# The rounding-down step of a fixed-point feed-forward block: an integer round trip, or a ladder of compares and subtractions

## The reference, cut to what matters

```python
x = L0_attn_x                                    # (4, 4096, 1024) fp32
x = x + _layernorm(_L0_attn_ref(_layernorm(x), Wq, Wk, Wv, Wo, bo))
x = x + _layernorm(_L0_ffn_ref(_layernorm(x), w1, b1, w2, b2))

def _L0_ffn_ref(x, w1, b1, w2, b2):              # w1 (1024, 4096), w2 (4096, 1024)
    h = x @ w1 + b1
    h = float2fix(h, 8)                          # round(h * 256) / 256
    h = pwlin_gelu_basic(h, 8, 8)                # 32 straight pieces of width 0.25 on [-4, 4]
    h = float2fix(h, 8)
    out = h @ w2 + b2
    return float2fix(out, 8)
```

## Time and profile before

| | us |
|---|---|
| median of 3 runs (7682.74 to 7688.47) | 7682.78 |
| the profiled execution | 7684.76 |
| its span, slowest core (core 4) | 7682.8 |
| spans of the 8 cores | 7658.8 to 7682.8 |
| VectorE busy | 2179.4 (28% of the span) |
| TensorE matmuls busy | 3020.9 (39%) |
| ScalarE busy | 1439.9 (19%) |

### The profile page before, as it was taken

How to read it: one execution, slowest core, us unless ns; L and a number is a source line. 1 busy time by engine, 2 the same in 40 slices (tenths; PEclk the granted TensorE clock), 3 DMA queues, 4 the chain that set the end, 5 groups by cost and what they waited for, 6 DMA issues and landing times.

```text
span 7682.8 us, 34600 instructions; the slowest of 8 cores (7658.8 to 7682.8 us)
## 1 busy us (share of the span) xinstructions
PE 3020.9 (39%) x7361; PEld 857.5 (11%) x7440; DVE 2179.4 (28%) x3496; ACT 1439.9 (19%) x2201; POOL 289.5 (4%) x484
## 2 busy tenths in 40 slices
PE   3434444444434444444444465222233332221443
PEld 1111000000011110000000111000000010000110
DVE  3331000000013320000000012577741137777112
ACT  1112222222211112222222200111110011111000
POOL 0000000000000000000000000000001100000110
PEclk7665555555556655555555555566555556655555
DMA  2110000000011110000000021111124431110443
GB/s 57 39 50 12 2 2 2 1 2 2 2 34 39 38 34 2 2 2 1 2 2 2 1 55 58 44 11 11 11 37 68 75 67 11 11 10 10 75 74 61
DMA packets 145193, 195.63 MB, mean 25 GB/s; under 512 B 77154, under 2 KB 87522, under 8 KB 144996
## 3 DMA queue, kind: packets, MB, share of 16 engines
q0 software_dynamic: 118272, 113.28, 9.8%
q1 hardware_dynamic: 26724, 80.14, 3.4%
HBM read 264.68 MB, written 20.97 MB: 37 GB/s over the span
## 4 chain that ended last, share of the span: by engine, by line
PE 32%; DVE 26%; ACT 18%; issue 11%; DMA 9%; DVEq 3%; ACTq 1%; POOL 0%; POOLq 0%; SPq 0%
ACT psbt L338 11%; PE pCp L362 9%; PE pSp L329 8%; DMA w2st<-w 7%; PE pMp L719 3%; PE pPp L268 3%; PE pWp L473 3%; PE pPp L289 3%; DVEq L79 2%; ACT sqscrt L180 2%; PE pZp L393 2%; DVE psbt L350 2%; PE pTp L251 1%; DVE xlt L195 1%; DVE statst L172 1%
## 5 line engine op out<-in xcount | busy, mean ns | idle before, releaser
L362 PE MATMUL pCp<-psbt,Vsb 128*65 128x512 bf16 (+3 forms) x1280 | 693.9, 542 | 1526.9 <-ACT psbt L338 880.1
L338 ACT ACTIVATE psbt<-pSp,biasmatt 128x512 bf16<-128x512 f32 (+3 forms) x1280 | 797.6, 623 | 2171.8 <-PE pSp L329 1871.7
L350 DVE TENSOR_TENSOR psbt<-psbt,maskst 128x128 bf16<-128x128 bf16 x512 | 115.4, 225 | 2554.4 <-ACT psbt L338 2554.4
L690 PE MATMUL pMp<-xlT2t,w1st 128*128 128x512 bf16 x1002 | 364.8, 540 | 1138.7 <-ACT c_ut L548 1132.7
L719 PE MATMUL pMp<-w2st,hqt 128*128 128x512 bf16 x1004 | 465.4, 616 | 696.8 <-DMA w2st<-w 611.5
L329 PE MATMUL pSp<-Qsb,Ksb 64*128 64x512 bf16 (+3 forms) x1280 | 690.0, 539 | 2.0 <-DVE biasmatt L315 2.0
L362 PEld LDWEIGHTS pCp<-psbt,Vsb 128*65 128x65 bf16 x1280 | 166.9, 130 | 2055.2 <-issue 2055.2
L180 ACT ACTIVATE sqscrt<-xstaget,statst 128x1024 f32<-128x1024 f32 x112 | 128.5, 1147 | 1138.1 <-DVE statst L175 1138.1
L251 PE MATMUL pTp<-identt,xlt 128*128 128x128 bf16 x768 | 97.1, 307 | 538.8 <-DVE xlt L195 538.8
L690 PEld LDWEIGHTS pMp<-xlT2t,w1st 128*128 128x128 bf16 x1024 | 129.1, 131 | 1374.0 <-issue 1347.3
L733 DVE SCALAR_TENSOR_TENSOR wosumt<-pMp,b_bt 128x512 f32<-128x512 f32 x32 | 20.6, 687 | 911.3 <-PE pMp L719 869.1
(11 more groups left out here) (89 smaller groups left out, 2879.2 us busy)
## 6 DMA issues: line engine op xcount, KB each, us to landing
w2st<-w POOLq DMA_DIRECT2D x256, 256.0 KB, 3.9
xstaget<-x_full SPq DMA_DIRECT2D x64, 512.0 KB, 3.5
xstaget<-x_my SPq DMA_DIRECT2D x48, 512.0 KB, 3.5
xstaget<-x2scr SPq DMA_DIRECT2D x32, 512.0 KB, 3.7
w1st<-w POOLq DMA_DIRECT2D x64, 256.0 KB, 4.6
x2scr<-x2tt POOLq DMA_DIRECT2D x16, 512.0 KB, 3.0
out<-outtt POOLq DMA_DIRECT2D x16, 512.0 KB, 4.7
ctxscr<-ctxstt POOLq DMA_DIRECT2D x64, 64.0 KB, 1.9
```

The source lines that it names most:

```text
L338: io.activation(out=psb[PB][:, C0:512], in_=pS[PB][:, C0:512], func=AF.Exp, bias=biasmat[:, KT:KT + 1], scale=0.125), sem="s")
L350: io.tensor_tensor(out=psb[PB][:, (SS - 4 * GG) * 128:(SS - 4 * GG + 1) * 128], in0=psb[PB][:, (SS - 4 * GG) * 128:(SS - 4 * GG + 1) * 128 ...
L362: io.matmul(pC[:, C0:512], Vsb[HH][:, KT * 65:KT * 65 + 65], psb[PB][:, C0:512], start=(KT == 0), stop=(KT == KM - 1)), sem="t")
L690: tm = op("tensor", lambda io, cc=c, HF=half, BUF=buf: io.matmul(pM[HF][:, 0:512], w1s[BUF][:, cc * 128:(cc + 1) * 128], xlT2[:, cc * 1024 ...
```

## The change

Each rounding down through an integer is replaced by a ladder that works in fp32 alone. A new helper `peel` takes a value buffer and a scratch buffer, and for each power of two C writes C·[v ≥ C] negated into the scratch (a `tensor_scalar`, L547 of the changed kernel) and adds it to the value (a `tensor_tensor`, L551), so that the value loses that bit. After the last level, 1, the fraction is left, and the floor is the source less the fraction. `ffn_chain` has 12 levels in each of its two places. In the first of them, after the 6 high levels, the rest is copied aside: it holds the low 6 bits and the fraction. The epilogue has 14 levels. The shifts that keep values positive become smaller (2048.5 for 16384.5), or, in the epilogue, larger (8192.5 for 0.5, and 32.0 is taken off again), so that the ladder covers the range.

```diff
-        for col, val in ((0, 1e-5), (1, -64.0), (2, -63.75), (3, 64.5), (4, 0.5)):
+        for col, val in ((0, 1e-5), (1, -8.0), (2, -7.75), (3, 64.5), (4, 8192.5)):
...
-            out=b1bias[:], in0=b1bias[:], scalar1=256.0, scalar2=16384.5,
+            out=b1bias[:], in0=b1bias[:], scalar1=256.0, scalar2=2048.5,
...
+        def peel(vbuf, bbuf, levels):
+            for c in levels:
+                op("vector", lambda io, C=c, V=vbuf, Bb=bbuf: io.tensor_scalar(
+                    out=Bb[:], in0=V[:], scalar1=float(C), scalar2=float(-C),
+                    op0=ALU.is_ge, op1=ALU.mult))
+                drain("vector")
+                op("vector", lambda io, V=vbuf, Bb=bbuf: io.tensor_tensor(
+                    out=V[:], in0=V[:], in1=Bb[:], op=ALU.add))
+                drain("vector")
...
-            op("vector", lambda io: io.tensor_copy(out=c_ti[:], in_=c_u[:]))
-            drain("vector")
-            op("vector", lambda io: io.tensor_copy(out=c_tf[:], in_=c_ti[:]))
-            drain("vector")
+            op("vector", lambda io: io.tensor_copy(out=c_e[:], in_=c_u[:]))
+            drain("vector")
+            peel(c_e, c_a, [2048, 1024, 512, 256, 128, 64])
+            op("vector", lambda io: io.tensor_copy(out=c_rf[:], in_=c_e[:]))
+            drain("vector")
+            peel(c_e, c_a, [32, 16, 8, 4, 2, 1])
             op("vector", lambda io: io.tensor_tensor(
-                out=c_e[:], in0=c_u[:], in1=c_tf[:], op=ALU.subtract))
-            drain("vector")
-            op("vector", lambda io: io.scalar_tensor_tensor(
-                out=c_a[:], in0=c_e[:], scalar=1.0, in1=c_tf[:],
-                op0=ALU.is_ge, op1=ALU.add))
-            drain("vector")
-            op("vector", lambda io: io.scalar_tensor_tensor(
-                out=c_nt[:], in0=c_e[:], scalar=0.0, in1=c_a[:],
-                op0=ALU.is_lt, op1=ALU.subtract))
-            drain("vector")
...
+                out=c_rf[:], in0=c_rf[:], in1=c_e[:], op=ALU.subtract))
+            drain("vector")
+            op("vector", lambda io: io.tensor_tensor(
+                out=c_tf[:], in0=c_u[:], in1=c_e[:], op=ALU.subtract))
             drain("vector")
             t_z = op("vector", lambda io: io.tensor_tensor(
-                out=c_z[:], in0=c_rf[:], in1=c_nt[:], op=ALU.add), sem="v")
+                out=c_z[:], in0=c_rf[:], in1=c_tf[:], op=ALU.subtract), sem="v")
...
+            op("vector", lambda io: io.tensor_copy(out=c_e[:], in_=c_u[:]))
+            drain("vector")
+            peel(c_e, c_a, [2048, 1024, 512, 256, 128, 64, 32, 16, 8, 4, 2, 1])
             op("vector", lambda io: io.tensor_tensor(
-                out=c_e[:], in0=c_u[:], in1=c_tf[:], op=ALU.subtract))
+                out=c_a[:], in0=c_u[:], in1=c_e[:], op=ALU.subtract))
...
-                    anchor_floor_1024(c_u)
+                    op("vector", lambda io: io.tensor_copy(out=c_e[:], in_=c_u[:]))
+                    drain("vector")
+                    peel(c_e, c_a, [8192, 4096, 2048, 1024, 512, 256, 128,
+                                    64, 32, 16, 8, 4, 2, 1])
+                    op("vector", lambda io: io.tensor_tensor(
+                        out=c_a[:], in0=c_u[:], in1=c_e[:], op=ALU.subtract))
+                    drain("vector")
                     op("vector", lambda io: io.tensor_scalar(
-                        out=lntmp[:], in0=c_nt[:], scalar1=-1.0 / 256, scalar2=0.0,
+                        out=lntmp[:], in0=c_a[:], scalar1=1.0 / 256, scalar2=-32.0,
                         op0=ALU.mult, op1=ALU.add))
```

More of the change, by code:

```diff
@@ L566, in ffn_chain @@
-            op("vector", lambda io: io.scalar_tensor_tensor(
-                out=c_nt[:], in0=c_e[:], scalar=0.0, in1=c_a[:],
-                op0=ALU.is_lt, op1=ALU.subtract))
-            drain("vector")
-            op("vector", lambda io: io.tensor_scalar(
-                out=c_ti2[:], in0=c_nt[:], scalar1=-1.0, scalar2=0.0,
-                op0=ALU.mult, op1=ALU.add))
-            drain("vector")
-            op("vector", lambda io: io.tensor_scalar(
-                out=c_ri[:], in0=c_ti2[:], scalar1=63, scalar2=0,
-                op0=ALU.bitwise_and, op1=ALU.bypass))
@@ L577, in ffn_chain @@
-            drain("vector")
-            op("vector", lambda io: io.tensor_copy(out=c_rf[:], in_=c_ri[:]))
+                out=c_tf[:], in0=c_u[:], in1=c_e[:], op=ALU.subtract))
             drain("vector")
             t_z = op("vector", lambda io: io.tensor_tensor(
-                out=c_z[:], in0=c_rf[:], in1=c_nt[:], op=ALU.add), sem="v")
+                out=c_z[:], in0=c_rf[:], in1=c_tf[:], op=ALU.subtract), sem="v")
             wait("scalar", "v", t_z)
             op("scalar", lambda io: io.activation(
-                out=c_g0[:], in_=c_z[:], func=AF.Gelu, bias=cbias[:, 1:2], scale=-1.0 / 256))
+                out=c_g0[:], in_=c_z[:], func=AF.Gelu, bias=cbias[:, 1:2],
@@ L585, in ffn_chain @@
+                scale=-1.0 / 256))
             drain("scalar")
             t_g = op("scalar", lambda io: io.activation(
-                out=c_g1[:], in_=c_z[:], func=AF.Gelu, bias=cbias[:, 2:3], scale=-1.0 / 256),
-                sem="s")
+                out=c_g1[:], in_=c_z[:], func=AF.Gelu, bias=cbias[:, 2:3],
+                scale=-1.0 / 256), sem="s")
             wait("vector", "s", t_g)
@@ L600, in ffn_chain @@
             t_u2 = op("scalar", lambda io: io.activation(
-                out=c_u[:], in_=c_y[:], func=AF.Identity, bias=cbias[:, 3:4], scale=256.0),
-                sem="s")
+                out=c_u[:], in_=c_y[:], func=AF.Identity, bias=cbias[:, 3:4],
+                scale=256.0), sem="s")
             wait("vector", "s", t_u2)
-            op("vector", lambda io: io.tensor_copy(out=c_ti[:], in_=c_u[:]))
+            op("vector", lambda io: io.tensor_copy(out=c_e[:], in_=c_u[:]))
             drain("vector")
-            op("vector", lambda io: io.tensor_copy(out=c_tf[:], in_=c_ti[:]))
-            drain("vector")
+            peel(c_e, c_a, [2048, 1024, 512, 256, 128, 64, 32, 16, 8, 4, 2, 1])
             op("vector", lambda io: io.tensor_tensor(
-                out=c_e[:], in0=c_u[:], in1=c_tf[:], op=ALU.subtract))
[L610 to L617, removed]
+                out=c_a[:], in0=c_u[:], in1=c_e[:], op=ALU.subtract))
             drain("vector")
             t_hq = op("vector", lambda io, FT=ft: io.tensor_scalar(
-                out=hq[:, FT * 1024:(FT + 1) * 1024], in0=c_nt[:],
-                scalar1=-1.0 / 256, scalar2=-0.25, op0=ALU.mult, op1=ALU.add),
+                out=hq[:, FT * 1024:(FT + 1) * 1024], in0=c_a[:],
+                scalar1=1.0 / 256, scalar2=-0.25, op0=ALU.mult, op1=ALU.add),
                 sem="v")
@@ L625, in ffn_chain @@
             return t_hq
[L627 to L643, removed]
         wait("sync", "x2a", cnt["x2a"])
```

## The result

| | median us | runs | ratio to before, 95% interval |
|---|---|---|---|
| before | 7684.61 (7682.74 to 7704.64) | 8 | |
| after | 10797.17 (10788.59 to 10801.51) | 8 | 1.4043 [1.4028, 1.4059] |

The change makes the kernel 3112.6 us slower, 40%. The forecast was 10827, in a range of 10780 to 10890. The profiled execution took 10807.74 us, its span 10805.6.

What follows compares the result with a forecast made beforehand. No engine bounds the whole; VectorE's chain is the path in the first loop and all 16 epilogues are exposed. 7684.8 + 3134 (turns 2724, epilogues 410) + 5 + 5 = 10829, put at 10827 us, range 10780 to 10890.

Steps and rivals of the forecast that it cites:

- VectorE's chain is on the path with its full length: First loop: every VectorE instruction between L548 and L619 counts in full; a turn 42.56 us longer, times 64, 2724 us.
- All 16 epilogues are exposed, by POOL's order: Second loop: stores ahead of w2 loads on POOL's queue expose both tiles' epilogues; 25.61 us each, times 16, 410 us.
- the rival's 7941: Second loop: second tile's epilogue hidden behind matmuls, 10 exposed; 7941 us for epilogues-only ladder, 10673 for the change, 2%.
- The prices, 694 and 1226 ns and 75 ns between: Ladder on VectorE: compare or copy 694 ns, two-tensor instruction 1226, gap 75; one level 2070 ns.
- The rival of the slow compare: Ladder: L547 runs at 1226 ns, 936 us more, 11763 us; 4%.
- rival of slow copies: Ladder's new copies on VectorE: 144 x 0.532 = 77 us more, 10904 us; 2%.
- Collisions, 5 us: First loop: POOL's w1 issue and VectorE's ladder instructions stretch each other; 5 us, bounds 0 and 28.
- the rule on the shared port: VectorE's copies, casts, tensor_scalar and GpSimd's descriptor generation wait for each other, tensor_tensor does not block; at most 28 us here.
- Hitches, 5 us: VectorE's 3024 added instructions: standing still for no visible reason, 5 us, below it 0.
- The clock, 0: Second loop: longer TensorE idleness ahead of it lowers the granted clock little; 19 us at most, charged 0.
- "ScalarE's work, TensorE's and the DMAs' are as before": Whole kernel: the change leaves the work of these engines and the loads' times as they were; nothing charged.
- the small terms: Collisions and hitches, 5 us each, added to the 3134 us of the turns and epilogues.

Runs made afterwards that it cites:

- e_magic: Kernel before with each rounding down replaced by adding and taking off 12582912 in fp32; 6844.65 us, ratio 0.8905.
- e_store: Changed kernel with the 16 output stores issued from SP's queue instead of POOL's; 10509.92 us, 287 less than the changed kernel.
- e_epi: Kernel before with the ladder in the 16 epilogues only, the first loop keeping the integer round trip; 8120.71 us, ratio 1.0573.
- e_fill_before: Kernel before with 378 useless memsets and drains per pair on VectorE, off the path, 3024 in all; 7655.19 us for 7686.72.
- the same kernel filled: `e_epi` with 328 useless memsets and drains per pair on VectorE, 2624 in all; 8066.97 us for 8120.71.
- the three filled kernels: Kernel before, `e_chain` and `e_epi`, each with useless memsets on VectorE up to the changed kernel's count; 7655.19, 10385.61 and 8066.97 us.
- e_chain: Kernel before with the ladder in both places of the first loop only, the epilogues keeping the integer round trip; 10425.81 us, ratio 1.3566.

## Why the prediction was right

- *VectorE's chain is on the path with its full length.* Right: a turn grew by 1323.9 / 31 = 42.7 us, with 42.56 predicted, and with fewer instructions it shrank as worked out (`e_magic`).
- *All 16 epilogues are exposed, by POOL's order.* Right, shown by `e_store` (287 us for 282) and by `e_epi`, where the rival's 7941 was 180 us off.
- *The prices, 694 and 1226 ns and 75 ns between.* Right, L547 at a mean of 696 included. The rival of the slow compare falls: 1760 x 0.532 us would have shown. The copies are at 694; the prediction had 144 of them in its rival of slow copies where there are 208 (3 x 64 + 16), so that this rival should have stood at 208 x 0.532 = 111 us more, 10938. L565 at 694 rules it out either way.
- *Collisions, 5 us.* L547's 1760 instructions took 1224.4 us, 3 more than at 694 ns each; the longest took 1084. Right in size. The trace also bears out the rule on the shared port as a mechanism, on the page's core. L547 was longer than 709 ns in 14 cases, all beside a w1 issue that had begun first, and each of the 14 ended 493 to 495 ns behind the end of the issue (the case above: 5048.71 and 5048.21). Where it was the w1 issue that grew, it ended 475 to 478 ns behind the end of an L547, in 14 cases, as here:

```profile
8299.67 0.69 DVE L547 TENSOR_SCALAR c_at<-c_et 128x1024 f32<-128x1024 f32 x1
8299.73 1.11 POOL L71 DMA_DIRECT2D w1st<-w  x1 [66.87 <-PE pMp L661]
```

  Distances that are the same whatever the overlap mean that one of the two waits until the other has let go; they don't both run on at a slower pace. None of the 1760 L551, with two tensors in, is lengthened, though 63 of them overlap an issue.
- *Hitches, 5 us.* The groups that are shown lost 5.6 and 5.1 us to them at L547 and L551 and 0.4 at L608, twice the estimate. What makes VectorE stand still there is not shown.
- *The clock, 0.* Right: 0.52 in the second loop before and after.
- *What was missed.* "ScalarE's work, TensorE's and the DMAs' are as before" was wrong for the DMAs. The second loop is paced in part by its loads, and these landed in 3.6 us for 3.9. The forecast difference was 3144 with the small terms; against a kernel before with a list of the same length it measured 3142. Against the real one it measured 3113, and the 30 us between are those of `e_fill_before` (31.5). The range, 10780 to 10890, had no term for this. The measured time lies inside because the loads gave 30 us and the lower bound was 47 us below the forecast; between `e_epi` and the same kernel filled they gave 54. So luck had a part in the time, not in the mechanism.

Why loads land sooner with this list of VectorE stays open. It is no matter of when VectorE works: in the three filled kernels the additions stand off the path, and the x loads are early before the first of them has run. The profile shows the instruction queue q14 with 124 packets before and 171 in the changed kernel and in all three filled ones. `e_epi` with 130 has the latest loads (4.1 us), `e_chain` with 165 lies at 3.9, and `e_magic` with 111, fewer than before, lies at 3.9 over the cores like before, so it is not steady in the length either: what the early ones have in common is the length of the changed kernel (171 or 172 packets). Where in memory the instructions and the weights lie is a guess that the runs can't confirm; the scratch tensor's length is excluded.

## What to carry to other kernels

When two engines hand one tile to and fro, price the edit by counting its instructions on that chain with the durations and gaps of like instructions, and ask in each stage what is queued behind the last of them: here the sum was good to what the runs can tell, some 10 us of 3142, once the loads' share was taken out. Replacing an exact but clumsy step pays in instructions, not in cleverness of types: 15 instructions a turn over integers beat 56 over floats, and 4 with an addition of a large constant beat both. A difference of half a per cent between two programs can come from instructions that do nothing and stand off the path; before a small part is explained by its mechanism, pad the other program to the same length. And read a median over all cores before saying that something did not move: the slowest core's page hid the x loads here.

## What the runs showed of the hardware that was not expected

3024 memsets of 59 ns with drains, where the engine idles, made the kernel 31.5 us faster (7655.19 for 7686.72, ratio 0.9955 [0.9941, 0.9970]), through w2 loads of 256 KB that land in 3.6 to 3.7 us for 3.9; loads of x land 0.3 us sooner as well, though the last of them is issued 3 ms ahead of the first memset. A VectorE instruction with one tensor in and an issue on POOL's queue wait for one another in turn: each of the 14 lengthened L547 ended 493 to 495 ns behind the issue, and they took up to 1084 ns for 694. An addition and removal of 12582912 in one `tensor_scalar` that writes int32 takes the ordinary 0.69 to 0.70 us (L555 of `e_magic`), and the compare ahead of a multiply in a `tensor_scalar` the ordinary 694 ns.
